# An attention and mixture-of-experts kernel on one core: six items ahead instead of eight, and the start reordered

## The chip, the cores and the metric

The kernel runs on one NeuronCore of a Trainium2 chip. The metric is the device time of one execution in microseconds. Engines are TensorE (PE, with its weight loads PEld), VectorE (DVE), ScalarE (ACT), GpSimd (POOL) and SyncE (SP), which here only issues DMAs.

## What is computed

x is 8 batches of 256 tokens of 128 channels. A layernorm gives xn. One branch is causal attention with 16 heads of 64 channels and rotary position, its keys and values made from a latent of 64 channels; the other is a router over 8 experts, of which each token uses one (hidden size 512, exact gelu). The result joins both.

```python
xn = _layernorm(x)
q = xn @ wq.T
lat = xn @ w_kv_down.T
k, v = lat @ w_k_up.T, lat @ w_v_up.T
s = softmax(causal(rope(q) @ rope(k).T / 8)) @ v @ wo.T
e = max(top2(xn @ gate_w + gate_b))
y = gelu(xn @ w1[e] + b1[e]) @ w2[e] + b2[e]
out = x + s * silu(2 * y)
```

## The kernel before

Every engine has its own program, written out by hand, and all follow one plan (`program`, L266): a start, then 64 slots g, one for each pair of heads of each batch (8 pairs in a batch), and between slots 39 and 40 (`G_LEAD`, L42) the experts, on tokens sorted by expert. Engines meet only at semaphores; each runs its own list in order.

An **item** m is one projection: 8 for each batch, alternately queries (even m) and keys (odd m) of four heads. PE makes it in `project` (L1011; 6 matmuls of 256 columns for queries, 4 for keys, because operands are split in a high and a low part of reduced precision), DVE multiplies it by cosine and sine in `rotate` (L552), POOL adds the two halves into `staged` in `rotated` (L434), and SP moves them with four DMAs for each pair of items (`place`, L343) into `qk_sb`, where the heads lie as the scores need them. One semaphore `qk_in` counts all four DMAs. In slot g PE makes the scores of g + 2 (`scores`, L1027), item g + 8 (`NI` is 8), transposes of the probabilities of g (`turn`, L1039), the output of g - 2 (`output`, L1062) and the values of g - 1 (`values`, L1049). So scores of pair of heads g, made in slot g - 2, need the items up to g + 1. Until slot 19 items use one PSUM bank, later two (`bank_of`, L326), so that a projection waits for the rotation of the item before it, or of the one before that.

In the slot DVE does in this order: row maxima of g + 2 (`row_max`, L559), reciprocals of g + 1, its share of the scaling, whatever stands in `slot` (L745) for that g (statistics in slots 0, 1, 4, 5, 7, 9, normalising of four tiles of tokens in slots 2, 6 and 10, routing in 17 to 22), and last the rotation. POOL scales the probabilities of g + 1 (`scale`, L443; two of the four parts in slots 22 to 37, else all four), adds item g + 8, and in slots 22 to 37 issues one indirect DMA each, which scatters a tile of tokens to its place in the sorted order. In slots 1, 5 and 9 it makes the power for a group of four tiles (`rstd`, L471).

The order on SP (`slot`, L406) is: in slot 39 wait for all scatters, load four tiles of sorted rows (`load`, L401, issue L403), wait for them, load the rest; then the moves, in odd slots; then in slots 1, 3 and 5 the experts' weights (`expert_weights`, L378): w1 in one DMA of 2 MB, w2 in four of 512 KB, b2 with a fill of the sorted array. On PE, `finish` (L1196) ends slot 39's work and transposes the first tile of sorted rows, and `experts` (L1206) waits for the weights, the tile's own weights (copied by POOL, `own_weights`, L516) and the rotations of items up to 47.

In the start (L349, L483, L693, L916, L1136) eight items are projected and rotated. The first four tiles of tokens are normalised and transposed, weights are split in high and low parts (ACT the high, DVE `query_low` L688 and POOL `key_low` L477 the low), value and output weights are multiplied together (`value_output_weights`, L1126), and the moves of items 0 and 1 are issued half by SP and half by ACT.

Of the kernel before, what the change touches and what calls it, by code (L numbers as in the profile page):

```python
# [16 lines left out]
P = 128  # L17
# [23 lines left out]
LEAD = 5  # L41
G_LEAD = LEAD * NP  # L42
# [9 lines left out]
Z_PART = 18  # L52

# [27 lines left out]
def build(nc, x, wqT, w_dgT, w_kupT, w_vup, woT, gate_b, w1, b1, w2, b2,  # L81
          c_rot, c_ident, c_mask, c_before, c_expert, c_excl, c_incl, c_tile, out):
    with ExitStack() as ctx:
# [76 lines left out]
        rstd_all = sb("rstd_all", [P, NT])  # L160
        lg = sb("lg", [P, NT, E])
# [30 lines left out]
        wk_in = [sem(f"wk_in{i}") for i in range(2)]  # L192
        wq_in_done = [sem(f"wq_in{i}") for i in range(2)]
# [11 lines left out]
        rstd_ready = sem("rstd_ready")  # L205
        xn_ready = sem("xn_ready")
# [29 lines left out]
        qk_in = [sem(f"qk_in{i}") for i in range(NG)]  # L236
# [55 lines left out]
        def latents_to(u):  # L292

            t0, t1 = TURNS[u]
            return (bank[1], bank[0], w_bank, w_bank, w_bank)[u][0:DW, 0:(t1 - t0) * P]
# [30 lines left out]
        def bank_of(m):  # L326

            return bank[4 + m % 2] if m < NI or m - NI >= TWO_J else j_bank
# [5 lines left out]
        def place_halves(eng, n, halves):  # L334

            for half in halves:
                for pair in range(2):
                    eng.dma_start(qk_sb[half::2, :, 2 * (n % NG) + pair, :],
                                  staged[HD * pair:HD * pair + HD, n % 2, half]).then_inc(qk_in[n % NG], 16)

        @block.sync
        def _(sp):
            def place(n, halves=(0, 1)):  # L343
# [3 lines left out]
                place_halves(sp, n, halves)  # L347

            def start():  # L349
# [18 lines left out]
                place(0, (0,))  # L368
# [4 lines left out]
                place(3)  # L373
# [4 lines left out]
            def expert_weights(k):  # L378
                if k == 0:
# [3 lines left out]
                    sp.dma_start(w1_view[:, :, 0:FF], w1.rearrange("e c f -> c e f")).then_inc(f_in, 16)  # L383
                    sp.dma_start(w1_view[:, :, FF:FW], b1).then_inc(f_in, 16)
                elif k == 1:
                    for i in range(FB):
# [19 lines left out]
            def slot(g):  # L406
# [26 lines left out]
        def _(pool):  # L433
            def rotated(m):  # L434
# [3 lines left out]
                if n >= 2:  # L438
                    pool.wait_ge(qk_in[(n - 2) % NG], 64 * ((n - 2) // NG + 1))
# [31 lines left out]
            def rstd(u):  # L471
# [3 lines left out]
                pool.tensor_tensor(rstd_all[:, n], veps[:, n], halfneg[:, n], op=ALU.pow).then_inc(rstd_ready, 1)  # L475
# [7 lines left out]
            def start():  # L483
# [7 lines left out]
                key_low(1)  # L491
                key_low(2)
                rotated(0)
                rotated(1)
                key_low(3)
                for m in range(2, 7):
                    rotated(m)
                scale(0)
                rotated(7)

            def slot(g):
                if g + 1 < B * NP and g != G_LEAD:
                    scale(g + 1)
                if g + NI < B * NP:
                    rotated(g + NI)
# [7 lines left out]
            def experts():  # L513
# [15 lines left out]
                pool.wait_ge(f_in, 16 * (2 + FB))  # L529
# [13 lines left out]
        def _(dve):  # L543
# [8 lines left out]
            def rotate(m):  # L552

                dve.wait_ge(proj_done, m + 1)
                wait(dve, staged_ready, m - 1)
# [41 lines left out]
            def variances(u):  # L597

                n = slice(*TURNS[u])
                dve.tensor_scalar(veps[:, n], mv[:, n, 1], LN_EPS, None, ALU.add).then_inc(var_ready, 1)  # L600

            def normalise(u):

                dve.wait_ge(rstd_ready, u + 1)
                for n in range(*TURNS[u]):
# [87 lines left out]
            def start():  # L693
# [9 lines left out]
                normalise(1)  # L703
# [570 lines left out]
```

## Time and profile before

| | us |
|---|---|
| median of 3 runs | 319.66 (319.2 to 320.86) |
| the profiled execution | 319.58 |
| its span, first to last instruction | 317.6 |
| PE busy | 292.8 (92%) |
| ACT busy | 240.7 (76%) |
| DVE busy | 221.0 (70%) |
| POOL busy | 217.4 (68%) |

Times in the rows are microseconds from the start of the span. A row of the timeline gives the start, the duration, the engine and the line, what is written from what, and in brackets how long the engine stood idle before it and who released it. "SPq" is a DMA issue. Slot g begins where PE makes the scores of g + 2 (L1034): slot 0 at 28.99, slot 1 at 31.41, slot 4 at 44.71, slot 39 at 177.22; the experts begin at 183.72.

### The profile page before, as it was taken

How to read it: one execution, taken by the hardware profiler on the slowest of the kernel's cores; microseconds unless marked ns; L12 is line 12 of the kernel's file. 1: busy time of each engine (PE TensorE's matmuls, PEld its weight loads, DVE VectorE, ACT ScalarE, POOL GpSimd, SP SyncE). 2: the span in 40 equal slices, each digit the busy share in tenths (PEclk: the TensorE clock that was granted, in tenths of full speed). 3: DMA queues.
4: the chain of work that ended last, by engine and by line, in shares of the span. 5: the costliest groups of instructions: out<-in, count | busy, mean ns of one | idle time of the engine just before them, and what ended most of it. 6: DMA issues, size and time to landing. Idle time of an engine off the chain costs nothing.

```text
span 317.6 us, 8745 instructions
## 1 busy us (share of the span) xinstructions
PE 292.8 (92%) x2485; PEld 244.6 (77%) x2485; DVE 221.0 (70%) x883; ACT 240.7 (76%) x863; POOL 217.4 (68%) x321
## 2 busy tenths in 40 slices
PE   0878889999999999999999989999999999999984
PEld 0756668787888888888888779999877887886853
DVE  4877898997869698877787522222268789997551
ACT  3226869787887779898999775555699997989972
POOL 3566967778677787999999943333138997899630
PEclk9968999999999999999999999999999999999998
DMA  7537499963333333344433470000063343344200
GB/s 205 188 88 179 105 293 253 311 180 68 67 70 68 67 69 76 86 107 114 104 92 85 107 218 3 0 2 0 2 179 72 87 103 95 101 130 131 59 18 19
DMA packets 39294, 33.37 MB, mean 105 GB/s; under 512 B 4753, under 2 KB 36370, under 8 KB 39250
## 3 DMA queue, kind: packets, MB, share of 16 engines
q1 hardware_dynamic: 37506, 30.24, 36.6%
q0 software_dynamic: 1024, 2.10, 2.6%
q10 hardware_dynamic: 720, 0.50, 0.6%
q8 instruction: 21, 0.34, 0.4%
q14 instruction: 23, 0.19, 0.2%
HBM read 11.07 MB, written 4.98 MB: 51 GB/s over the span
## 4 chain that ended last, share of the span: by engine, by line
PE 73%; issue 8%; DVE 8%; POOL 7%; ACT 2%; DMA 1%; ACTq 1%; POOLq 0%; DVEq 0%
PE bank L1046 11%; PE bank L1034 10%; PE bank L1057 9%; PE bank L1071 8%; PE bank L1235 6%; PE bank L1220 6%; PE bank L1023 4%; PE bank L1036 3%; PE bank L1007 3%; PE bank L1059 3%; POOL staged L440 3%; DVE rot_out L556 3%; PE bank L1024 2%; PE bank L1008 2%; PE bank L1009 2%
## 5 line engine op out<-in xcount | busy, mean ns | idle before, releaser
L852 ACT ACTIVATE pexp<-masked,negmax 128x128 f32<-128x128 f32 (+1 forms) x256 | 114.6, 454 | 3.3 <-DVE negmax L565 3.2
L565 DVE CUSTOM_DVE_ANT_0 masked<-bank,mask 128x128 f32<-128x128 f32 (+1 forms) x256 | 76.0, 353 | 32.4 <-PE bank L1036 32.0
L440 POOL TENSOR_TENSOR staged<-rot_out 128x512 f32<-128x512 f32 x64 | 82.1, 1284 | 23.7 <-DVE rot_out L556 20.8
L451 POOL TENSOR_SCALAR probs<-pexp,rden 128x256 f32<-128x256 f32 (+1 forms) x186 | 80.7, 449 | 23.1 <-DVE rden L572 20.7
L556 DVE TENSOR_TENSOR rot_out<-bank,rot 128x1024 f32<-128x1024 f32 x64 | 77.8, 1215 | 1.5 <-PE bank L1009 0.8
L873 ACT COPY probsT<-bank 128x384 f32<-128x384 f32 x128 | 54.9, 480 | 28.0 <-PE bank L1046 26.8
L1046 PE MATMUL bank<-ident,probs 128*128 128x128 f32 x384 | 53.9, 274 | 0.7 <-POOL probs L451 0.3
L852 ACT ACTIVATION_READ_ACCUMULATOR pexp<-masked,negmax 128x1 f32 x256 | 50.1, 196 | 0.0
L1034 PE MATMUL bank<-qk_sb 64*128 64x256 f32 x256 | 45.5, 432 | 1.9 <-ACT vo_sb L946 1.2
L1046 PEld LDWEIGHTS bank<-ident,probs 128*128 128x128 f32 x384 | 43.2, 140 | 3.0 <-POOL probs L451 1.0
L1071 PE MATMUL bank<-vo_sb,ctxT 128*128 128x128 f32 x256 | 39.9, 278 | 2.7 <-ACT ctxT L879 2.7
L1057 PE MATMUL bank<-probsT,lat_all 128*64 128x256 f32 x256 | 41.8, 404 | 0.3 <-ACT probsT L873 0.3
L991 ACT ACTIVATE hidT<-bank,w_own 128x128 f32<-128x128 f32 x88 | 25.1, 368 | 18.5 <-PE bank L1220 18.4
L1071 PEld LDWEIGHTS bank<-vo_sb,ctxT 128*128 128x128 f32 x256 | 33.8, 191 | 4.3 <-ACT ctxT L879 3.8
L520 POOL COPY w_own<-w_sb 128x516 f32 x22 | 13.5, 616 | 27.3 <-ACT hidT L991 27.3
L1034 PEld LDWEIGHTS bank<-qk_sb 64*128 64x128 f32 x256 | 19.5, 186 | 13.0 <-issue 10.5
L1036 PEld LDWEIGHTS bank<-qk_sb 64*128 64x128 f32 x256 | 25.1, 189 | 3.0
L879 ACT COPY ctxT<-bank 128x256 f32<-128x256 f32 x64 | 23.3, 364 | 4.9 <-PE bank L1059 4.9
L1059 PEld LDWEIGHTS bank<-probsT,lat_all 128*64 128x64 f32 x256 | 18.4, 137 | 9.2
L1235 PE MATMUL bank<-w_sb,hidT 128*128 x176 | 24.4, 282 | 1.0 <-issue 0.5
L1036 PE MATMUL bank<-qk_sb 64*128 64x128 f32 x256 | 25.1, 273 | 0.0
L1059 PE MATMUL bank<-probsT,lat_all 128*64 128x128 f32 x256 | 24.9, 273 | 0.0
(106 smaller groups left out, 457.8 us busy)
## 6 DMA issues: line engine op xcount, KB each, us to landing
qk_sb<-staged SPq DMA_DIRECT2D x126, 128.0 KB
w_sb<-in_w SPq DMA_DIRECT2D x1, 2048.0 KB, 8.7
w_sb<-in_w SPq DMA_DIRECT2D x4, 512.0 KB, 6.2
sorted_x<-z SPq DMA_DIRECT2D x1, 1408.0 KB, 9.9
sorted_g<-z SPq DMA_DIRECT2D x1, 1152.0 KB, 5.9
out<-res SPq DMA_DIRECT2D x8, 128.0 KB
x_sb<-in_x SPq DMA_DIRECT2D x3, 256.0 KB, 3.3
rot<-in_c_rot SPq DMA_DIRECT2D x1, 512.0 KB, 5.8
```

The costliest lines, as they stand in the source:

```text
L440: pool.tensor_tensor(staged[:, n % 2, :, m % 2, :], rot_out[:, m % 2, :, 0:S], rot_out[:, m % 2, :, S:2 * S], op=ALU.add).then_inc(staged_ ...
L451: pool.tensor_scalar(probs[:, g % 2, i, c], pexp[:, g % 2, i, c], rden[:, g % 2, i, k:k + 1], 1.0, ALU.mult, ALU.mult).then_inc(probs_read ...
L556: dve.tensor_tensor(rot_out[:, m % 2], bank_of(m)[:].unsqueeze(1).broadcast_to([P, 2, 2 * S]), rot[:], op=ALU.mult).then_inc(rope_done, 1)
L565: t = dve.tensor_tensor_reduce(masked[:, g % 2, i, c], s_bank[i][:, c], mask[:, c], -1.0, -NEG * 1e8, ALU.add, ALU.min, negmax[:, g % 2, i ...
L852: e = act.activation(pexp[:, g % 2, i, c], masked[:, g % 2, i, c], ACT.Exp, bias=negmax[:, g % 2, i, k:k + 1], scale=-1.0, accum_out=rowsu ...
L873: act.copy(probsT[:, g % 2, i, :], t_bank[i][:, 0:SW]).then_inc(probsT_ready, 1)
L1034: pe.matmul(s_bank[i][:, P:SW], qk_sb[r, 0, p, P:S], qk_sb[r, 1, p, :], start=True, stop=True)
L1036: m = pe.matmul(s_bank[i][:, 0:P], qk_sb[r, 0, p, 0:P], qk_sb[r, 1, p, 0:P], start=True, stop=True)
L1046: t = pe.transpose(t_bank[i][:, k * P:(k + 1) * P], probs[:, g % 2, i, k * P:(k + 1) * P], ident[:])
L1057: pe.matmul(o_bank[r, 0:S], lat_all[:, 2 * b, :], probsT[:, g % 2, i, 0:S], start=True, stop=False)
L1059: m = pe.matmul(o_bank[r, P:S], lat_all[:, 2 * b + 1, :], probsT[:, g % 2, i, S:SW], start=False, stop=True)
L1071: m = pe.matmul(y_bank[:, i * C:(i + 1) * C], ctxT[:, p, i * P:(i + 1) * P], vo_sb[:, p, :], start=(p == 0 and i == 0), stop=(p == NP - 1) ...
```

## The change

Six items are projected in the start (`AHEAD`) instead of eight. In slot g every engine does the items `items(g)`: one, g + 6; but in slots 36 and 38 (`TWICE`) two, so that 48 items are done before the experts, as before. PE does a second item at the end of the slot. `qk_in` becomes one semaphore for each pair of heads, signalled by its two DMAs. All four moves of the first pair are on SP. The expert weights come in pieces of half of w1, or half of w2, in slots 1, 3, 5 and 7, and b2 and the fill in slot 9. In slots 2, 6 and 10 ACT normalises two of the four tiles, from a shift (minus mean times power) that POOL computes behind the power. In the start, PE runs 13 matmuls on ones ahead of everything and 4 behind the first transposes; wq and wk are loaded in three pieces each; item 1 is summed by DVE; the order of the steps is new on each engine; half of the first scaling is DVE's.

```diff
+AHEAD = 6
+TWICE = (36, 38)
+def items(g):
+    ahead = [AHEAD + sum(t < n for t in TWICE) for n in (g, g + 1)]
+    return range(g + ahead[0], min(g + 1 + ahead[1], B * NP))
...
-        qk_in = [sem(f"qk_in{i}") for i in range(NG)]
+        qk_in = [sem(f"qk_in{p}") for p in range(NP)]
...
-            if g >= B * NP - 3:
+            if g == 0 or g >= B * NP - 3:
...
-            return bank[4 + m % 2] if m < NI or m - NI >= TWO_J else j_bank
+            return bank[4 + m % 2] if m < NI or m - AHEAD >= TWO_J else j_bank
...
-            def place(n, halves=(0, 1)):
+            def place(n):
                 sp.wait_ge(staged_ready, 2 * n + 2)
                 wait(sp, scores_done, 2 * n + 2 - NP)
-                place_halves(sp, n, halves)
+                for pair in range(2):
+                    p = 2 * (n % NG) + pair
+                    for half in range(2):
+                        sp.dma_start(qk_sb[half::2, :, p, :],
+                                     staged[HD * pair:HD * pair + HD, n % 2, half]).then_inc(qk_in[p], 16)
...
-                sp.dma_start(rot[:], c_rot).then_inc(rot_in, 16)
-                sp.dma_start(wq_in[:, S:], wqT[:, S:]).then_inc(wq_in_done[1], 16)
-                sp.dma_start(wkup[:, S:], w_kupT[:, S:]).then_inc(wk_in[1], 16)
+                for i in range(1, 3):
+                    c = slice(i * S, (i + 1) * S if i == 1 else H * HD)
+                    sp.dma_start(wq_in[:, c], wqT[:, c]).then_inc(wq_in_done[i], 16)
+                    sp.dma_start(wkup[:, c], w_kupT[:, c]).then_inc(wk_in[i], 16)
+                    if i == 1:
+                        sp.dma_start(rot[:], c_rot).then_inc(rot_in, 16)
...
-                place(0, (0,))
+                place(0)
                 place(1)
                 rows_in(3)
                 place(2)
                 rows_in(4)
-                place(3)
...
-                if g % 2 and g + NI < B * NP:
-                    place((g + NI) // 2)
-                if g in (1, 3, 5):
+                for m in items(g):
+                    if m % 2:
+                        place(m // 2)
+                if g in (1, 3, 5, 7, 9):
                     expert_weights(g // 2)
...
-                pool.tensor_tensor(rstd_all[:, n], veps[:, n], halfneg[:, n], op=ALU.pow).then_inc(rstd_ready, 1)
+                    pool.tensor_tensor(rstd_all[:, n], veps[:, n], halfneg[:, n], op=ALU.pow).then_inc(pool_step, 1)
+                    pool.wait_ge(pool_step, u - 1)
+                    pool.tensor_tensor(shift_all[:, n], negmean[:, n], rstd_all[:, n], op=ALU.mult).then_inc(rstd_ready, 1)
...
                 key_low(1)
+                rotated(0)
                 key_low(2)
-                rotated(0)
-                rotated(1)
+                rotated(2)
+                rotated(3)
                 key_low(3)
-                for m in range(2, 7):
+                for m in range(4, AHEAD - 1):
                     rotated(m)
                 scale(0)
-                rotated(7)
+                rotated(AHEAD - 1)
...
                 turned_low(0)
-                normalise(1)
+                query_low(1)
                 latents_low(0)
                 dve.wait_ge(rot_in, 16)
                 rotate(0)
-                query_low(1)
+                rotate(1)
+                dve.wait_ge(rope_done, 2)
+                dve.tensor_tensor(staged[:, 0, :, 1, :], rot_out[:, 1, :, 0:S], rot_out[:, 1, :, S:2 * S],
+                                  op=ALU.add).then_inc(staged_ready, 1)
+                normalise(1)
+                rotate(2)
                 turned_low(1)
-                rotate(1)
                 query_low(2)
-                rotate(2)
+                rotate(3)
                 latents_low(1)
-                rotate(3)
-                query_low(3)
-                rotate(4)
-                rotate(5)
...
                 row_max(0)
-                rotate(6)
+                rotate(4)
                 row_max(1)
                 denominators(0)
-                rotate(7)
+                scale(0)
+                query_low(3)
+                rotate(5)
                 logits(0)
...
-                    normalise(2)
+                    normalise(2, 2, 4)
...
+                if g in (2, 6, 10):
+                    normalise(g // 4 + 2)
...
-                if p % 2 == 0:
-                    pe.wait_ge(qk_in[p // 2], 64 * (g // NP) + 64)
+                pe.wait_ge(qk_in[p], 32 * (g // NP) + 32)
...
+            def keep_warm(n):
+                for _ in range(n):
+                    pe.matmul(y_bank[:], ones16[:], ones16[:].unsqueeze(1).broadcast_to([P, 4, P]), start=True, stop=True)
...
+                pe.wait_ge(hot_ready, 1)
+                keep_warm(13)
                 pe.wait_ge(id_in, 16)
                 turn_rows(0)
+                keep_warm(4)
                 latents(0)
...
-                if g + NI < B * NP:
-                    project(g + NI)
+                if g < 2:
+                    wait(pe, wq_low if g == 0 else wk_low, 4)
+                for m in items(g)[:1]:
+                    project(m)
...
+                for m in items(g)[1:]:
+                    project(m)
...
-                pe.wait_ge(rope_done, NI * (LEAD + 1))
+                pe.wait_ge(rope_done, items(G_LEAD)[0])
```

PE's start now runs: items 0 to 3, the transposes of tiles 2 and 3, half of the value-output weights, their latents, the other half, scores 0, item 4, scores 1, item 5. ACT's start copies the value-output weights before the first exponentials and turned latents after them. `rotate` and `rotated` are called for `items(g)` on DVE and POOL, as on PE.

## Rows read from the trace of the kernel before

**Rows 1.** Busy time by stretch: stretch, length, PE, PEld, DVE, ACT, POOL, PE clock, DMA share, GB/s.
```profile
10.16:29.00 18.84, 14.14 (x97) 11.31 (x95) 15.39 (x31) 6.26 (x21) 12.45 (x13) 0.82 0.50 129
29.00:49.10 20.10, 17.53 (x149) 14.30 (x149) 17.71 (x83) 15.46 (x58) 16.20 (x29) 1.00 0.71 191
18.60:25.40 6.80, 6.44 (x32) 5.54 (x34) 6.01 (x13) 1.91 (x8) 5.60 (x5) 0.50 0.39 90
128.00:158.00 30.00, 30.00 (x266) 25.05 (x263) 23.13 (x96) 26.74 (x104) 28.17 (x36) 1.00 0.41 104
```

**Rows 2.** Timeline of the start: start, us, engine, line, operation, names, shapes, count.
```profile
5.83 0.41 DVE L685 SCALAR_TENSOR_TENSOR wq_l<-w_sb,wq_h 128x256 fp32r<-128x256 f32 x1
...
8.56 0.41 PE L1007 MATMUL bank<-xnT_h,wq_h 128*128 128x256 f32 x1
...
10.16 1.23 DVE L556 TENSOR_TENSOR rot_out<-bank,rot 128x1024 f32<-128x1024 f32 x1 [0.54 <-PE bank L1009]
...
11.26 1.59 POOL L481 TENSOR_TENSOR wk_l<-w_sb,wk_h 128x256 fp32r<-128x256 f32 x2 [3.17 <-ACT wk_h L914]
11.30 0.97 DVE L685 SCALAR_TENSOR_TENSOR wq_l<-w_sb,wq_h 128x256 fp32r<-128x256 f32 x1
...
12.90 0.28 PE L1008 MATMUL bank<-xnT_l,wq_h 128*128 128x256 f32 x1
...
28.99 0.70 PE L1034 MATMUL bank<-qk_sb 64*128 64x256 f32 x4 [1.17 <-ACT vo_sb L946]
...
29.96 0.29 DVE L565 CUSTOM_DVE_ANT_0 masked<-bank,mask 128x128 f32<-128x128 f32 x1 [0.85 <-PE bank L1036]
```

**Rows 3.** Timeline of slots 1 to 7, the steps around the normalising.
```profile
37.81 1.02 POOL L475 TENSOR_TENSOR rstd_all<-veps,halfneg 128x4 f32<-128x4 f32 x1
...
38.86 1.66 DVE L606 TENSOR_SCALAR xn<-x_sb,mv,rstd_all 128x128 f32<-128x128 f32 x4 [1.19 <-POOL rstd_all L475]
...
41.70 0.38 PE L1023 MATMUL bank<-latT,wk_h 128*128 128x256 f32 x1 [1.43 <-DVE rot_out L556]
...
58.61 0.39 PE L1023 MATMUL bank<-latT,wk_h 128*128 128x256 f32 x1 [0.54 <-DVE rot_out L556]
```

**Rows 4.** Timeline of PE: the first matmuls of slots 36, 37 and 38.
```profile
166.47 0.70 PE L1034 MATMUL bank<-qk_sb 64*128 64x256 f32 x4
...
170.13 0.70 PE L1034 MATMUL bank<-qk_sb 64*128 64x256 f32 x4
...
173.56 0.70 PE L1034 MATMUL bank<-qk_sb 64*128 64x256 f32 x4
```

**Rows 5.** Timeline of POOL before the experts.
```profile
171.73 1.06 POOL L459 DMA_INDIRECT sorted_x<-xn,pos  x1 [0.16 <-issue]
172.83 0.93 POOL L451 TENSOR_SCALAR probs<-pexp,rden 128x256 f32<-128x256 f32 x2
...
176.47 1.62 POOL L451 TENSOR_SCALAR probs<-pexp,rden 128x128 f32<-128x128 f32 x4
...
182.38 1.17 POOL L520 COPY w_own<-w_sb 128x516 f32 x2
```

**Rows 6.** Timeline of SP's queue before the experts, and PE's first transpose of sorted rows.
```profile
175.25 2.55 SPq L338 DMA_DIRECT2D qk_sb<-staged  x4
178.59 3.53 SPq L403 DMA_DIRECT2D z<-sorted_x  x2
...
182.63 0.33 PE L1194 MATMUL bank<-ident,z 128*128 128x128 f32 x1
```

**Rows 7.** Timeline: moves and who waits for them; slot 25's first matmul and its moves.
```profile
21.69 2.98 SPq L338 DMA_DIRECT2D qk_sb<-staged  x4
26.60 1.28 POOL L440 TENSOR_TENSOR staged<-rot_out 128x512 f32<-128x512 f32 x1 [2.26 <-DMA qk_sb<-staged]
...
127.61 0.70 PE L1034 MATMUL bank<-qk_sb 64*128 64x256 f32 x4
133.60 16.40 SPq L338 DMA_DIRECT2D qk_sb<-staged  x12
```

More of the change, by code:

```diff
@@ L191, in build @@
         c_in = sem("c_in")
-        wk_in = [sem(f"wk_in{i}") for i in range(2)]
-        wq_in_done = [sem(f"wq_in{i}") for i in range(2)]
+        wk_in = [sem(f"wk_in{i}") for i in range(3)]
+        wq_in_done = [sem(f"wq_in{i}") for i in range(3)]
         gb_in = sem("gb_in")
@@ L437, in rotated @@
                 pool.wait_ge(rope_done, m + 1)
-                if n >= 2:
-                    pool.wait_ge(qk_in[(n - 2) % NG], 64 * ((n - 2) // NG + 1))
+                for q in (2 * n - 4, 2 * n - 3) if n > 1 else ():
+                    pool.wait_ge(qk_in[q % NP], 32 * (q // NP) + 32)
                 pool.tensor_tensor(staged[:, n % 2, :, m % 2, :], rot_out[:, m % 2, :, 0:S], rot_out[:, m % 2, :, S:2 * S],
@@ L503, in slot @@
                     scale(g + 1)
-                if g + NI < B * NP:
-                    rotated(g + NI)
+                for m in items(g):
+                    rotated(m)
                 if SCATTER_SLOT <= g < SCATTER_SLOT + NT:
@@ L554, in rotate @@
                 dve.wait_ge(proj_done, m + 1)
-                wait(dve, staged_ready, m - 1)
+                wait(dve, staged_ready, max(m - 1, 2) if m > 1 else 0)
                 dve.tensor_tensor(rot_out[:, m % 2], bank_of(m)[:].unsqueeze(1).broadcast_to([P, 2, 2 * S]), rot[:],
@@ L599, in variances, with normalise @@
                 n = slice(*TURNS[u])
+                if u > 1:
+                    dve.tensor_scalar(negmean[:, n], mv[:, n, 0], -1.0, None, ALU.mult)
                 dve.tensor_scalar(veps[:, n], mv[:, n, 1], LN_EPS, None, ALU.add).then_inc(var_ready, 1)
-            def normalise(u):
+            def normalise(u, first=0, last=TQ):
                 dve.wait_ge(rstd_ready, u + 1)
-                for n in range(*TURNS[u]):
+                for n in range(*TURNS[u])[first:last]:
                     dve.tensor_scalar(xn[:, n, :], x_sb[:, n, :], mv[:, n, 0:1], rstd_all[:, n:n + 1],
@@ L806, in slot @@
                     finalise(FINALS[g])
-                if g + NI < B * NP:
-                    rotate(g + NI)
+                for m in items(g):
+                    rotate(m)
             def finish(b):
@@ L902, in latents_copied, with normalise @@
                          src[:, 0:TQ * LAT]).then_inc(lat_copied, 1)
+            def normalise(u):
+                act.wait_ge(rstd_ready, u + 1)
+                for n in range(*TURNS[u])[0:2]:
+                    act.activation(xn[:, n, :], x_sb[:, n, :], ACT.Identity, bias=shift_all[:, n:n + 1],
+                                   scale=rstd_all[:, n:n + 1]).then_inc(xn_ready, 1)
             def query_high(i):
                 c = w_part[i]
-                act.wait_ge(wq_in_done[min(i, 1)], 16)
+                act.wait_ge(wq_in_done[min(i, 2)], 16)
                 act.mul(wq_h[:, c], wq_in[:, c], HD ** -0.5).then_inc(wq_high, 1)
@@ L923, in start @@
                 key_high(0)
+                turned(0)
+                query_high(1)
+                key_high(1)
+                latents_high(0)
+                turned(1)
+                query_high(2)
+                key_high(2)
                 act.wait_ge(id_in, 16)
@@ L1011, in project @@
             def project(m):
-                b, n, g = m // NI, m % NI, m - NI
-                wait(pe, rope_done, m if 0 <= g <= TWO_J else m - 1)
+                b, n, g = m // NI, m % NI, m - AHEAD
+                wait(pe, rope_done, m if m >= NI and g <= TWO_J else m - 1)
                 if g == TWO_J + 1:
@@ L1082, in turn_rows @@
                 for k, n in enumerate(range(*TURNS[u])):
-                    pe.wait_ge(xn_ready, n + 1)
+                    pe.wait_ge(xn_ready, n + 1 if u < 2 else TURNS[u][1])
                     t = pe.transpose(turned_to(u)[:, k * P:(k + 1) * P], xn[:, n, :], ident[:])
```

73 lines of the change are left out of this document (31 added, 42 removed).

## The prediction

> **What bounds the kernel now.** I read four views in this order. The busy time by stretch [rows 1] says where TensorE (PE) is short of work: it is busy 30.00 of 30 us in the middle of the attention slots, but 14.14 of 18.84 in the second part of the start and 17.53 of 20.1 in the first five slots. A microsecond of PE work moved is therefore worth a microsecond in the middle, and next to nothing in the start. The timeline of the start [rows 2] shows what the first slot waits for: its scores go at 28.99, after 8 rotations of 1.23 us on VectorE (DVE) one after the other, and the last release is a copy on ScalarE (ACT). DVE is busy 15.39 of those 18.84 us [rows 1]: it is the engine that paces the start, with 3.45 us idle. The timeline of slots 1 to 7 [rows 3] shows the same engine holding PE: the key projection waits 1.43 us for a rotation at 41.70 and 0.54 us at 58.61, each time because four normalisations (1.66 us) stand ahead of the rotation. The timeline before the experts [rows 5, 6] shows GpSimd (POOL) with hardly a gap (28.17 of 30 us busy in the middle [rows 1]). Some half a per cent, 1.6 us, is what a measurement of this kernel can tell from no change.
>
> The profiled execution took 319.58 us, its span 317.6; the median of the runs shown is 319.66. I make the sum against 319.6.
>
> **1. The start, up to DVE's first slot.** Until the first rotation little moves: DVE follows the arrival of x and POOL's power, both unchanged. The 13 warm-up matmuls run before PE has anything else to do. The products before the first rotation now run at 1.2 GHz, those after it at 2.4: 0.41 and 0.28 us for one of 256 columns [rows 2], of which the columns are 0.21 and 0.11. If the 13 warm-ups of 512 columns all ran at 1.2 GHz they would take 13 × 0.43 = 5.5 us and push the first transposes 0.8 us back; if the clock rises on the way, they end in time. Then the three latent and six query products save about 0.1 each, and the rotation at 10.16 [rows 2] starts at about 9.3, where the table it needs (its load is one of those queued later by 256 KB, some 0.8 us) arrives too.
> From there I add DVE's work. Before: 15.39 us busy to 29.0 [rows 1]. It loses two rotations (2 × 1.23) and a 0.97 us split that now comes before the first rotation; it gains two normalisations moved behind it (0.6), the sum of item 1 (bounded below by half of a 1024-element rotation, 0.6, and above by POOL's time for the same sum, 1.28 [rows 7]; I take 0.65, since a DVE shape is nearer than a POOL one), and half of the first scaling (0.6). That is 13.8 us. Idle time: walking the new order by hand, DVE waits for the first scores, because their moves can only start when two sums are done (at about 12.4) and land 3.2 us later, and again for the second scores; I get 1.3 us. So DVE reaches its first slot at 9.3 + 13.8 + 1.3 = 24.4 where it now gets there at 29.96 [rows 2]: **−5.5 us**. Ends: no idle at all −6.8, all of the present 3.45 us kept −3.3. Two projections taken from PE's start save nothing themselves; PE had 4.7 us free there [rows 1].
> Here the trace has a row on two engines at once: the 256-column split on DVE takes 0.97 us at 11.30 while POOL runs the same kind of subtraction from 11.26, 0.80 each, and 0.41 at 5.83 with POOL idle [rows 2]. The Trainium skill (SBUF — State Buffer, Who interferes with whom) states why: a VectorE instruction with two SBUF inputs and a GpSimd one that reads SBUF lock the same port pair, and the later one waits in full. By that rule DVE's new sum waits for POOL's sum of item 0 beside it, and the start would come out up to 1.3 us later, the sum below at −1.55 in place of −2.85; POOL's sum starts 1.2 us earlier, so I leave it out.
>
> **2. First slots.** Slots 0 to 3 stay paced by DVE, so the shift of 5.5 is kept. Two of the four normalisations of each group go to ACT: 0.83 us off DVE, and about 0.2 us back for POOL's extra small product that both now wait for (no row has it; between 0.1 and the 1.02 of the power beside it [rows 3]). In slot 2 that gives another **−0.3** once PE is no longer waiting for the rest, and in slots 6 and 10 it removes the wait of 0.54 us [rows 3]: **−1.1** for the two. ACT has the room (15.46 busy of 20.1 [rows 1]). The expert weights come as 1 MB at a time behind the moves of every second slot instead of 2 MB at once; nobody waits for them now, so nothing there.
>
> **3. The two projections come back.** In slots 36 and 38 PE does one projection more, a key and a query one. An even slot (query, 6 matmuls) lasts 3.66 us and an odd one (key, 4) 3.43 [rows 4]: 0.115 per matmul, so 0.46 + 0.69 = **+1.15**, in full on the path.
>
> **4. What the extra sums do to POOL and to SP's queue.** This is the term the diff hides. POOL has no gap in slots 35 to 37: a scatter issue (1.06), two scalings (0.93), one sum (1.28 [rows 5, 7]). Now slot 36 has two sums, and the second waits for a rotation of a projection that PE does last in its slot, at 170.7 in the old times, rotated by 172.0: the scatter at 171.73 [rows 5] goes to 173.5, the next to 176.9. In slot 38 come the four scalings (1.62 [rows 5]) and then both sums, 45 and 46. The moves of item pair 22 wait for sum 45; they went at 175.25 [rows 6] and now go at about 180.9. They are ahead of the load of sorted rows on SP's queue: four issues, 2.55 us [rows 6], so the load that went at 178.59 goes at 183.5 and lands at 186.2. PE transposed its first tile at 182.63 [rows 6] and with the 1.15 of part 3 would want it at 183.8: **+2.4**. The second load waits for the first, which adds about **+0.5** at the second tile. POOL's weight copy, 182.38 [rows 5], goes to about 185.1; it is covered by that wait. Ends: nothing, if POOL has slack I don't see; +4 if the walk is a microsecond short.
>
> **Sum:** −5.5 − 0.3 − 1.1 + 1.15 + 2.4 + 0.5 = −2.85; **316.8 us**.
>
> **Rivals.** (a) The clock falls again. It was at half from 18.6 to 25.4, with PE busy 6.44 of 6.8 us [rows 1]. There is no warm-up work after the first products, and PE still has pauses between them. In the new order what lies on the path from there to DVE's first slot is one projection and two sets of scores, some 1.6 us more: 318.4. (b) POOL and SP keep up before the experts: part 4 is nothing, 313.9. For it: POOL's period is a little below PE's, so it may have more lead by slot 36 than the rows show. (c) The start's idle time doesn't shrink, because the moves and splits that DVE waits for only change places: −3.3 in place of −5.5, 319.0; the change then does not do what it says. (d) Slower: with six items ahead the moves come too late. An odd slot's moves must be down three slots later, 3.43 + 3.66 + 3.43 = 10.52 us [rows 4]. In slot 37 they start 5.1 us after the slot [rows 4, 6]; landing took 1.9 us after the last issue (24.67 to 26.60, [rows 7]), so a first pair is down 3.2 after its start: 8.3. But in slot 25 they start 6.0 us after it (127.61 to 133.60 [rows 7]), beside a scatter. If landings under scatters take 1.5 us more, each of some eight pairs in slots 23 to 37 holds PE by 0.5 to 1; at 2 us more it is about 8 × 1.0 = 8 us, and the time 324. It decides from 1.3 us more. Against it: the signal is now by pair, so the second pair's landing no longer counts.
>
> **Chances.** Forecast 0.40, (a) 0.20, (b) 0.20, (c) 0.12, (d) 0.08. Faster by over 0.5% means under 318.1: nearly all of the forecast, a third of (a), all of (b), hence 0.67. Within 0.5%: 0.25. Slower by over 0.5%: 0.08, (d). The range goes from (b) to (c) with the bounds of parts 1 and 4: 313.5 to 319.6. It leaves out (d) and the outer ends of the others.
>
> **What would show it.** Right: scores of slot 0 near 22 and of slot 4 near 39; a half-clock row gone or not tells (a); no wait in slots 7 and 11; the load of sorted rows nearly 5 us later against slot 36 than now, with PE's first expert transpose waiting for it. Wrong: PE waiting for moves in even slots from 24 on (d), a load that goes right after the last scatter (b), slot 0 at 24 or later at full clock (c).

## The result: 1.6 us faster, where 2.8 had been forecast

| | before | changed |
|---|---|---|
| median of 10 runs each, us | 319.43 (318.29 to 320.86) | 317.87 (317.22 to 318.16) |
| the profiled execution | 319.58 | 317.84 |

The ratio is 0.9953, 95% interval 0.9938 to 0.9968: faster by 1.56 us, just under half a per cent. The first slot starts 7.6 us earlier, and four fifths of that are lost again by the time the experts end. The first lines of the page of the changed kernel:

```profile
span 316.1 us, 8823 instructions
PE 296.5 (94%) x2502; PEld 244.6 (77%) x2502; DVE 217.2 (69%) x883; ACT 243.0 (77%) x869; POOL 215.9 (68%) x321
```

PE is busier (296.5 us for 292.8) though its work is the same but for the 17 warm-up matmuls, whose products nobody uses. The account is best kept by the time at which PE begins a slot, which is a row of its timeline (L1064 for L1034 before). Negative numbers are the change against before.

| slot | 0 | 4 | 13 | 36 | 39 | 40 |
|---|---|---|---|---|---|---|
| before | 28.99 | 44.71 | 82.91 | 166.47 | 177.22 | 230.07 |
| changed | 21.37 | 37.75 | 74.99 | 158.56 | 170.88 | 228.60 |
| difference | -7.62 | -6.96 | -7.92 | -7.91 | -6.34 | -1.47 |

So there are three stretches to explain: a gain of 7.9 up to slot 13, a loss of 1.6 in slots 36 to 38, and a loss of 4.9 from slot 39 to 40, where the experts lie. After slot 40 nothing changes.

**The start.** Timeline of the changed kernel, from its first matmuls to DVE's first slot; it answers to [rows 2]:

```profile
1.10 5.67 PE L1169 MATMUL bank<-ones 128*128 128x512 bf16 x13 [1.10 <-DVE ones L716]
...
9.42 2.35 DVE L576 TENSOR_TENSOR rot_out<-bank,rot 128x1024 f32<-128x1024 f32 x2
...
10.72 1.28 POOL L454 TENSOR_TENSOR staged<-rot_out 128x512 f32<-128x512 f32 x1 [1.91 <-DVE rot_out L576]
...
11.81 0.75 DVE L731 TENSOR_TENSOR staged<-rot_out 128x512 f32<-128x512 f32 x1
...
14.46 0.41 DVE L707 SCALAR_TENSOR_TENSOR wq_l<-w_sb,wq_h 128x256 fp32r<-128x256 f32 x1
14.55 0.91 POOL L500 TENSOR_TENSOR wk_l<-w_sb,wk_h 128x256 fp32r<-128x256 f32 x1 [2.54 <-ACT wk_h L945]
...
21.37 0.70 PE L1064 MATMUL bank<-qk_sb 64*128 64x256 f32 x4 [1.00 <-DVE negmax L585]
...
21.94 0.41 DVE L707 SCALAR_TENSOR_TENSOR wq_l<-w_sb,wq_h 128x256 fp32r<-128x256 f32 x1
...
23.50 0.27 DVE L585 CUSTOM_DVE_ANT_0 masked<-bank,mask 128x128 f32<-128x128 f32 x1
```

The first rotation goes at 9.42 for 10.16, and DVE reaches the row maximum of its first slot at 23.50 for 29.96. Each split of a query weight takes 0.41 us on DVE, where those of before took 0.97, 0.73 and 1.30. Busy time by stretch, with the columns of [rows 1]:

```profile
9.42:23.50 14.08, 11.78 (x102) 9.53 (x103) 12.74 (x34) 8.23 (x29) 7.77 (x8) 1.00 0.65 174
```

DVE is busy 12.74 of these 14.08 us and idle 1.34. The granted clock (the column before the last two, as a share of 2.4 GHz) is 1.00 throughout; before, it was 0.50, which is 1.2 GHz or half clock, from 18.6 to 25.4.

**Slots 2 to 7**, timeline, answering to [rows 3]:

```profile
30.12 0.38 PE L1038 MATMUL bank<-xnT_h,wq_h 128*128 128x256 f32 x1 [1.13 <-DVE rot_out L576]
...
31.39 1.02 POOL L492 TENSOR_TENSOR rstd_all<-veps,halfneg 128x4 f32<-128x4 f32 x1
...
32.48 0.20 POOL L494 TENSOR_TENSOR shift_all<-negmean,rstd_all 128x4 f32<-128x4 f32 x1
...
32.72 0.88 ACT L932 ACTIVATE xn<-x_sb,shift_all,rstd_all 128x128 f32<-128x128 f32 x2 [0.34 <-POOL shift_all L494]
32.72 0.84 DVE L628 TENSOR_SCALAR xn<-x_sb,mv,rstd_all 128x128 f32<-128x128 f32 x2 [1.46 <-POOL shift_all L494]
...
34.74 0.38 PE L1054 MATMUL bank<-latT,wk_h 128*128 128x256 f32 x1 [0.88 <-DVE rot_out L576]
...
51.18 0.39 PE L1054 MATMUL bank<-latT,wk_h 128*128 128x256 f32 x1
```

PE's wait in slot 3 is 0.88 for 1.43, and that of slot 7 is gone. But DVE now stands 1.46 us for POOL's small product, where it stood 1.19 for the power.

**Slots 36 to 40**, timeline, answering to [rows 4 to 6]: PE's first matmuls of slots 36 to 39, POOL, SP's queue, and PE's two waits behind:

```profile
158.56 0.70 PE L1064 MATMUL bank<-qk_sb 64*128 64x256 f32 x4
...
162.89 0.70 PE L1064 MATMUL bank<-qk_sb 64*128 64x256 f32 x4
...
166.55 0.70 PE L1064 MATMUL bank<-qk_sb 64*128 64x256 f32 x4
...
169.19 1.06 POOL L473 DMA_INDIRECT sorted_x<-xn,pos  x1 [0.17 <-issue]
...
170.29 1.62 POOL L465 TENSOR_SCALAR probs<-pexp,rden 128x128 f32<-128x128 f32 x4
...
170.88 0.70 PE L1064 MATMUL bank<-qk_sb 64*128 64x256 f32 x4
...
171.89 2.51 POOL L454 TENSOR_TENSOR staged<-rot_out 128x512 f32<-128x512 f32 x2
...
173.19 2.55 SPq L354 DMA_DIRECT2D qk_sb<-staged  x4
...
175.78 3.83 SPq L416 DMA_DIRECT2D z<-sorted_x  x2
...
178.86 0.75 SPq L416 DMA_DIRECT2D z<-sorted_x  x1
178.93 0.30 PE L1231 MATMUL bank<-ident,z 128*128 128x128 f32 x1 [2.56 <-DMA z<-sorted_x]
...
187.63 1.15 PE L1272 MATMUL bank<-w_sb,hidT 128*128 x8 [1.35 <-ACT hidT L1022]
```

Slots 36 and 38 last 4.33 us each. The load of sorted rows goes at 175.78, 4.90 us after the start of slot 39 (before: 178.59, 1.37 after it), right behind the four moves; PE waits 2.56 us for it. The second load, of the remaining rows, is issued at 178.86, once the first has landed, and lands 8.6 us later, at 187.5. The product of the second tile (`experts`, where t is 1) waits in the program for both loads; it goes at 187.63, and the ACT operation that it needs had ended at 185.4. So this wait of 1.35 us is for the second load. Between the two waits the granted clock falls for a while:

```profile
176.30:180.70 4.40, 1.45 (x12) 1.25 (x11) 0.77 (x3) 2.54 (x6) 2.91 (x6) 0.99 0.44 107
180.70:184.10 3.40, 3.02 (x15) 2.57 (x13) 0.29 (x1) 1.14 (x4) 1.37 (x3) 0.50 0.95 281
```

### The profile page after: what moved, and what is told of

The parts are those of the page before. It is cut to its first block, busy times and chain, and to the rows that moved or that the text cites. A ratio compares the mean times of both kernels' runs of the same rounds, so it can differ in the third digit from the quotient of the medians.

```text
span 316.1 us, 8823 instructions
## 1 busy us (share of the span) xinstructions
PE 296.5 (94%) x2502; PEld 244.6 (77%) x2502; DVE 217.2 (69%) x883; ACT 243.0 (77%) x869; POOL 215.9 (68%) x321
## 4 chain that ended last, share of the span: by engine, by line
PE 63%; DVE 11%; issue 11%; POOL 10%; ACT 2%; DMA 2%; SPq 1%; POOLq 0%; DVEq 0%; ACTq 0%
PE bank L1076 9%; PE bank L1064 8%; PE bank L1087 7%; PE bank L1101 6%; PE bank L1257 6%; PE bank L1272 6%; POOL staged L454 5%; DVE rot_out L576 4%; DVE masked L585 3%; POOL probs L465 3%; PE bank L1038 3%; PE bank L1089 3%; PE bank L1066 3%; PE bank L1054 2%; PE bank L1169 2%
## 5 line engine op out<-in xcount | busy, mean ns | idle before, releaser
L454 POOL TENSOR_TENSOR staged<-rot_out 128x512 f32<-128x512 f32 x63 | 80.4, 1277 | 23.9 <-DVE rot_out L576 23.3
L1064 PE MATMUL bank<-qk_sb 64*128 64x256 f32 x256 | 45.0, 428 | 2.7 <-DVE negmax L585 2.5
L1064 PEld LDWEIGHTS bank<-qk_sb 64*128 64x128 f32 x256 | 19.4, 184 | 13.7 <-issue 12.6
L1257 PE MATMUL bank<-xsT,w_own 128*128 128x128 f32 x176 | 24.7, 286 | 0.8 <-DVE xsT L845 0.8
```

The lines of the kernel that those rows point to most:

```text
L454: pool.tensor_tensor(staged[:, n % 2, :, m % 2, :], rot_out[:, m % 2, :, 0:S], rot_out[:, m % 2, :, S:2 * S], op=ALU.add).then_inc(staged_ ...
L1064: pe.matmul(s_bank[i][:, P:SW], qk_sb[r, 0, p, P:S], qk_sb[r, 1, p, :], start=True, stop=True)
L1257: m = pe.matmul(bank[4 + o][:, k * P:(k + 1) * P], w1_own[:, o, k * P:(k + 1) * P], xsT[:, o, :], start=True, stop=True)
```

## The experiments

Twelve kernels were run, in five rounds each beside the kernel before, whose median was 319.3 to 320.1. Starts of slots and times, in us:

| kernel | slot 0 | slot 13 | slot 39 | slot 40 | median (lowest to highest) | ratio to before, 95% |
|---|---|---|---|---|---|---|
| e1 loads first | 21.53 | 75.17 | 171.05 | 224.33 | 313.75 (313.11 to 314.02) | 0.9810 (0.9781 to 0.9839) |
| e2 catch up at 20, 22 | 21.39 | 75.01 | 171.10 | 225.39 | 314.27 (313.71 to 314.64) | 0.9823 (0.9794 to 0.9852) |
| e3 warm in the wait | 21.02 | 74.66 | 170.54 | 227.60 | 317.31 (316.87 to 317.56) | 0.9924 (0.9899 to 0.9949) |
| e4 normalise on DVE | 21.33 | 77.36 | 173.25 | 230.32 | 319.74 (319.15 to 321.56) | 1.0011 (0.9991 to 1.003) |
| e5 e1, no warm-ups | 22.54 | 76.20 | 172.08 | 225.51 | 314.64 (313.77 to 315.88) | 0.9846 (0.9818 to 0.9875) |
| e6 e1, item 1 on POOL | 22.57 | 77.08 | 172.96 | 226.35 | 315.19 (313.69 to 315.80) | 0.9849 (0.9818 to 0.9880) |
| e7 e1 and e2 | 21.11 | 74.74 | 170.82 | 224.38 | 313.88 (313.61 to 314.07) | 0.9823 (0.9799 to 0.9847) |
| e8 before, warm-ups | 26.67 | 81.22 | 175.53 | 228.34 | 318.67 (317.53 to 320.18) | 0.9971 (0.9951 to 0.9992) |
| e9 before, ACT moves nothing | 27.08 | 81.01 | 175.31 | 227.97 | 317.54 (316.04 to 319.00) | 0.9929 (0.9905 to 0.9952) |
| e10 e1, eight ahead | 24.56 | 77.77 | 172.07 | 225.66 | 315.16 (314.12 to 315.78) | 0.9849 (0.9814 to 0.9885) |
| e11 e1, power first | 21.59 | 74.13 | 170.01 | 223.44 | 312.44 (312.09 to 313.12) | 0.9767 (0.9734 to 0.9800) |
| e12 e1, weights whole | 21.32 | 78.33 | 174.21 | 227.76 | 314.33 (313.90 to 317.01) | 0.9822 (0.9790 to 0.9854) |

### e1: the loads of sorted rows ahead of the moves

```diff
                     load(4, NR)
+                    for m in items(g - 1):
+                        if m % 2:
+                            place(m // 2)
                 for m in items(g):
-                    if m % 2:
+                    if m % 2 and g != G_LEAD - 2:
                         place(m // 2)
```

> SP issues the two loads of sorted rows ahead of the moves of items 44 and 45, no other edit. Theory (the queue: moves ahead of the loads, and the second load sets when the second tile's product may go): the first load goes within 1 us of the last scatter's landing, about 172.5 instead of 175.8, PE waits at most 0.3 us before the first transposed tile, the clock stays at full, slot 40 comes 3 us earlier than in the changed kernel: about 314.8 us in all. Rival (POOL is what is late; its copies of the experts' weights bind): the load moves but PE then waits for the weight copy at 177.8 instead, and at most 1 us is won: 317. Rival (the half clock costs the time, and comes from something other than the wait): the clock row stays and less than 1 us is won.

313.75 us, 4.1 less than the changed kernel. Timeline:

```profile
171.72 3.46 SPq L416 DMA_DIRECT2D z<-sorted_x  x2
...
175.28 7.53 SPq L354 DMA_DIRECT2D qk_sb<-staged  x8
176.47 0.33 PE L1234 MATMUL bank<-ident,z 128*128 128x128 f32 x1
...
178.12 1.13 PE L1260 MATMUL bank<-xsT,w_own 128*128 128x128 f32 x8 [0.41 <-POOL w_own L543]
```

The load goes 0.67 us after slot 39's start, PE's transpose waits for nothing, its clock stays at 2.4 GHz, and slot 39 to 40 takes 53.28 us for 57.72 (before: 52.85). The order on one issue queue is worth 4.4 us here; what is left over before is 0.4, the wait for POOL's weight copy. The second load goes at 174.43 and lands 7.0 us later, 1.9 before PE's product of the second tile wants it, so it holds nothing. The time is 1 us under the forecast.

### e2: the two extra items in slots 20 and 22

```diff
-TWICE = (36, 38)
+TWICE = (20, 22)
```

> The two extra items are projected in slots 20 and 22 instead of 36 and 38. Theory (POOL has no slack in the slots with scatters, and has some before them): the two sums are absorbed before slot 36, the loads stand to slot 39 as in the kernel before, and the end is at 319.6 - 7.9 + 1.2 to 1.6 = about 313 us. Rival (the extra items cost wherever they are, since DVE has its routing work in slots 17 to 22): stalls of 1 to 3 us in slots 20 to 24, 315 to 317. Rival (a later start of the scatters in slot 22 keeps POOL late to the end): about 316.

314.27 us. POOL and SP catch up before the scatters, the load goes at 172.34, and slot 39 to 40 takes 54.29. The two extra projections cost the same in either place: slot 39 starts at 171.10 for 170.88. PE still waits 0.75 us for this load, which takes 5.0 us from its issue to the transpose, for 3.15 in the changed kernel, and then 0.89 us for the second load. The forecast of 313 left out both.

### e3: warm-up matmuls in the wait for the load

```diff
                     pe.wait_ge(masked_ready, 2 * G_LEAD + 4)
+                    for _ in range(11):
+                        pe.matmul(bank[1][:], ones16[:],
+                                  ones16[:].unsqueeze(1).broadcast_to([P, 4, P]), start=True, stop=True)
                     pe.wait_ge(xs_in, 16)
```

> PE runs 11 matmuls on ones (about 2.4 us at full clock, into a bank that is free) while it waits for the first load; the loads stay where they are. Theory (the second load sets the time of the second tile's product): the clock stays at full and the first tiles go faster by 1.5 us, but the second product waits that much longer, and the time stays within 0.3 us of the changed kernel, 317.6 to 318.2. Rival (the fall of the clock is what costs): about 1.4 us faster, 316.4.

317.31 us, 0.56 less than the changed kernel; slot 39 to 40 takes 57.06 us, 0.66 less. The granted clock is 1.00 throughout, and PE comes to the second tile's product earlier, but then waits for the second load all the same:

```profile
186.63 1.15 PE L1274 MATMUL bank<-w_sb,hidT 128*128 x8 [0.90 <-issue]
```

So the theory on the second load holds: in the changed kernel PE's slower work at half clock is hidden in front of that landing. The 0.66 us come from the landing itself: it is 7.0 us after the issue, for 8.6, but the issue is 0.8 us later, because the first load took that much longer (transpose 3.94 us after its issue, for 3.15). Without that delay the quicker landing would be worth about 1.4. Over all profiled executions the second load landed 6.8 to 7.1 us after its issue, except in the changed kernel (8.6) and e4 (8.2), the only two with half clock at that place. That the clock makes the load slower is not shown.

### e4: all four tiles normalised on DVE

The slots' `normalise(u, 2, 4)` on DVE take all four tiles, ACT none; POOL's shift stays.

> DVE normalises all four tiles of each group again, ACT none; POOL still computes the shift. Theory (the share that ACT took removes PE's wait of 0.54 us in slots 7 and 11 and some of that in slot 3): slots 7 and 11 have their wait back, slot 13 begins about 1.5 us later than in the changed kernel (74.99), and the end is about 1.5 us later, 319.4. Rival (ACT's share only moves work; the wait was covered by the first slots' chain): less than 0.4 us.

319.74 us, 1.9 more than the changed kernel and as slow as the kernel before. Slot 13 starts 2.37 us later, in three steps of 0.8 (slots 3, 7 and 11). In slot 3 PE waits twice as long as with the work shared:

```profile
35.50 0.39 PE L1053 MATMUL bank<-latT,wk_h 128*128 128x256 f32 x1 [1.68 <-DVE rot_out L576]
```

In slots 7 and 11 it waits 0.79 us each, for 0.54 in the kernel before and nothing in the changed one.

### e5 and e8: the warm-up matmuls, taken away and added

e5 is e1 without both calls of `keep_warm`; e8 is the kernel before with both.

> The kernel with the loads first (313.75 us), without the 13 and the 4 warm-up matmuls. Theory (the clock in the start is a part of the gain): the first rotation begins at about 10.1 instead of 9.4, and the clock falls to half for a stretch of the start as in the kernel before; DVE paces the start, so only the two scores and projections on its path get longer: 1.5 to 2.5 us slower in all, about 315.8. Rival (the order alone made the gain, the clock none): within 0.7 us, the shift of the first rotation. Rival (the clock made most of it): over 4 us slower.

> The kernel before with the 13 and the 4 warm-up matmuls at the same places, nothing else. Theory (the old order has its own waits on ACT and DVE, the clock is a lesser part): the first rotation at 9.4 instead of 10.16, no half-clock stretch, slot 0 about 1.5 to 2.5 us earlier than 28.99, the time about 317.4. Rival (the clock made most of the 7.6 us that the start won): slot 0 at 24 or earlier, 314 or so. Rival (nothing, as the clock falls all the same behind the warm-ups): within 0.8 us.

Without them e1 takes 314.64 us, 0.9 more: slot 0 starts 1.0 later. Its products of 256 columns still take 0.41 us at 13.00, the pace of 1.2 GHz, and 0.28 from 15.9 on, where e1 has 0.28 from 8.5 us on. (The granted clock of the profile reads 1.00 in this stretch too; the pace is read from the durations.) The half-clock stretch that was forecast does not come: the granted clock stays at 1.00 up to 309. With them the kernel before takes 318.67, a ratio of 0.9971 or 0.9 us less (slot 0 starts 2.3 us earlier in the profiled execution, which at 317.76 is one of the fastest of twelve). DVE's first rotation goes at 8.98 for 10.16 there, and the half-clock stretch is shorter (19.0 to 22.4). So the warm-ups give about a microsecond in either kernel, and e1 has no half-clock stretch in the start with them or without.

### e6: item 1 summed by POOL

```diff
-                dve.wait_ge(rope_done, 2)
-                dve.tensor_tensor(staged[:, 0, :, 1, :], ...).then_inc(staged_ready, 1)
...
                 rotated(0)
+                rotated(1)
                 key_low(2)
```

> The kernel with the loads first, with item 1's two halves added by POOL behind item 0's instead of by DVE. Theory (the sum on DVE lets the first moves start early, at the price of 0.75 us of DVE): the first moves start 0.75 us later (POOL ends at 13.3), DVE is 0.7 us ahead until it waits for the first scores; slot 0 within 0.5 us, either way. Rival (the first moves set the start): slot 0 0.8 us later or more.

Not settled. The six executions lie at 313.7 and 313.9, with a mean granted clock of 1.00, and at 314.9 to 315.8 (four), with 0.987 to 0.994. In the profiled one, of the second group, slot 0 starts 1.04 us later than in e1: PE waits 2.21 us for moved items there, where it waits 0.99 for DVE in e1, and the clock is at 1.2 GHz from 22.2, near the end of that wait, to 29.0. So slot 0 is late by what the rival asked for, but not for its reason: SP's first four moves go at 12.77 for 12.74, and in the second four one issue takes 1.61 us, the others 0.6. Why that one is long is not known. In the two executions of the first group the time is that of e1, so there DVE's sum neither costs nor gives more than a few tenths.

### e7: e1 and e2 together

> Loads first and the extra items in slots 20 and 22. Theory (what was left of e2_twice_20_22 is the second load, which waits for moves issued ahead of the first; with these behind it the experts start as in the kernel with loads first, and the earlier items cost 0.2 us more before slot 39): 313.6 to 314.0, the same as loads first alone. Rival (POOL is still late with the extra sums at 36 and 38, and its slack counts now): 0.5 us or more faster than 313.75.

313.88 us for 313.75: nothing on top. Once the loads go first, what POOL and SP still owe is behind them and costs nothing.

### e9: the kernel before with ACT issuing no moves

```diff
-                place(0, (0,))
+                place(0)
...
-                act.wait_ge(staged_ready, 2)
-                place_halves(act, 0, (1,))
```

> The kernel before, with all four moves of items 0 and 1 issued by SP and none by ScalarE. Theory (in the start before, ScalarE stands 5.44 us idle in front of the copy of the latents at 17.23 because its queue holds two moves that wait for both staged items, and VectorE then waits 2.11 us for that copy at 17.63): the copy goes as soon as its matmul is done, near 14, VectorE's wait of 2.11 goes, slot 0 starts about 2 us earlier (near 27) and the time is near 317.5. Rival (the moves themselves pace the start: with four issues on one queue the last lands some 1.3 us later, and TensorE at half clock has its own work to do): slot 0 moves by less than 0.5 us and the time stays within 0.5 us of the kernel before.

317.54 us. In the kernel before, the timeline has:

```profile
15.55 1.63 ACTq L338 DMA_DIRECT2D qk_sb<-staged  x2
...
17.23 0.37 ACT L889 CAST latT<-bank 64x256 fp32r<-64x256 f32 x1 [5.44 <-issue]
...
17.63 0.42 DVE L619 TENSOR_TENSOR latT<-bank,latT 64x256 fp32r<-64x256 f32 x1 [2.11 <-ACT latT L889]
```

and in e9:

```profile
13.72 0.37 ACT L889 CAST latT<-bank 64x256 fp32r<-64x256 f32 x1 [2.11 <-PE bank L1007]
...
15.42 5.90 SPq L338 DMA_DIRECT2D qk_sb<-staged  x8
```

The copy goes 3.5 us earlier, DVE no longer waits for it, slot 0 starts 1.9 us earlier, and the time falls by 0.7%, or 2.3 us. (Half clock lasts from 20.2 to about 23.7 here, for 18.6 to 25.4; what share of the gain that is was not tried.) Two DMAs on an engine's queue, waiting for items of other engines, had held the engine's own work.

### e10: eight items ahead again

```diff
-AHEAD = 6
-TWICE = (36, 38)
+AHEAD = 8
+TWICE = ()
```

with items 6 and 7 projected and rotated in the start, and their moves, on e1.

> The changed kernel with the loads of sorted rows ahead of the last moves (as e1_loads_first), eight items ahead instead of six, and so no slot with two projections. Theory (the start is paced by VectorE's work; rotations of items 6 and 7, 1.2 us each, come back into it, and the two extra projections in slots 36 and 38 cost 1.6 us): slots from 4 to 36 start about 2.4 us later than with six, 1.6 us come back by slot 40, and the time is 314.5 against 313.75. Rival 1 (the number ahead is most of what the change gains in the start, through the wait chain and not only the two rotations): more than 3 us slower, 317 or over. Rival 2 (the start has room on VectorE and TensorE for both): the slots start where they start with six, and the time is 312.2.

315.16 us, 1.4 over e1. Slots 4 to 36 start 2.60 us later (161.33 for 158.73 at slot 36), and 1.58 come back in slots 36 and 38. The edit changes the number ahead alone, but its price has the clock in it: before item 6 PE waits 1.91 us for the split query weights, and half clock lasts from the end of that wait, 22.1, to 25.5. Five of the six executions have a mean granted clock of 0.986 to 0.994 and take 314.6 to 315.8; the one with 0.998 takes 314.12, 0.4 over e1.

### e11: POOL's power ahead of the sum

```diff
+                if g in (1, 5, 9):
+                    rstd(2 + g // 4)
                 for m in items(g):
                     rotated(m)
...
-                if g in (1, 5, 9):
-                    rstd(2 + g // 4)
```

> As e1_loads_first, with POOL's power and its small product for the next four tiles issued ahead of that slot's sum, in slots 1, 5 and 9, in place of behind it. Theory (in slot 2 VectorE waits 1.46 us for that small product at 32.72, and TensorE 0.88 us for the rotation behind it at 34.74): both waits go, slots from 4 on start 0.9 to 1.4 us earlier, and the time is near 312.6 against 313.75. Slots 6 and 10, where TensorE did not wait, give nothing. Rival (POOL has no slack: the sum that now stands behind 1.2 us of power holds the moves and the next rotation, and TensorE waits as long at another place): slot 13 starts within 0.3 us of where it does in e1_loads_first, and so does the end.

312.44 us, the best kernel of the study: 2.3% under the kernel before, or about 7.5 us. Timeline of slots 1 to 3:

```profile
29.84 1.01 POOL L495 TENSOR_TENSOR rstd_all<-veps,halfneg 128x4 f32<-128x4 f32 x1
...
30.93 0.20 POOL L497 TENSOR_TENSOR shift_all<-negmean,rstd_all 128x4 f32<-128x4 f32 x1
31.08 1.27 POOL L457 TENSOR_TENSOR staged<-rot_out 128x512 f32<-128x512 f32 x1
...
31.40 1.38 DVE L631 TENSOR_SCALAR xn<-x_sb,mv,rstd_all 128x128 f32<-128x128 f32 x2
...
34.00 0.39 PE L1057 MATMUL bank<-latT,wk_h 128*128 128x256 f32 x1
```

DVE's wait of 1.46 and PE's of 0.88 are gone; slot 4 starts 0.91 earlier than in e1 and slot 13 1.04.

### e12: the expert weights whole

w1 as one DMA of 2 MB in slot 1, the four of w2 in slot 3, the rest in slot 5.

> As e1_loads_first, with the expert weights loaded as in the kernel before: w1 as one DMA of 2 MB in slot 1, the four of w2 in slot 3, the rest in slot 5. Theory (with six ahead instead of eight the moves of slots 3 and 5 have only three slots to land, and they queue behind bursts of 2 MB): TensorE stalls up to 1.5 us in slots 6 to 10 waiting for a moved item, slot 13 starts that much later, and the time is 313.8 to 315. Rival (loading in pieces changes nothing that anyone waits for, as forecast): no wait for a move in slots 4 to 12, slot 13 and the time within 0.3 us of e1_loads_first.

314.33 us, 0.6 over e1. The timeline shows the moves of slot 5 behind the four DMAs of w2, and PE's wait for them in slot 8:

```profile
42.39 5.38 SPq L397 DMA_DIRECT2D w_sb<-in_w  x4
47.87 3.65 SPq L354 DMA_DIRECT2D qk_sb<-staged  x4
```

```profile
55.91 0.70 PE L1064 MATMUL bank<-qk_sb 64*128 64x256 f32 x4 [1.69 <-DMA qk_sb<-staged]
```

In the profiled run, the slowest of the seven at 317.01 (the others take 313.9 to 314.9, so their wait or what follows it must be smaller), this wait is followed by half clock:

```profile
57.50:60.90 3.40, 3.40 (x16) 2.92 (x14) 2.43 (x16) 1.43 (x3) 2.48 (x5) 0.50 1.07 303
```

So loading in pieces matters with six ahead. The kernel before loads whole with eight ahead, and in its trace PE waits for no move: there the moves had two slots more.

## Why the prediction was right, and where its sizes were off

The direction, the steps and their places were right; the parts came to -1.5 at slot 40 for a forecast of -2.85. That it is no further off is in part luck: the start gained 1.0 us more than forecast, and the stretch before and in the experts lost 2.4 more.

**Part 1, forecast -5.5 at DVE's first slot, measured -6.5.** The first rotation (9.3 forecast, 9.42) and the idle time (1.3 forecast, 1.34) were right. The term that was mis-sized is DVE's work, 13.8 forecast and 12.74 measured. It kept the splits of query weights at the durations of before, 0.73 and 1.30 us; they took 0.41 each, 1.2 less in all. By the Trainium skill (SBUF — State Buffer, Who interferes with whom) the one of two such instructions that comes later waits. The rows agree on which: at 14.46 DVE's split came 0.09 us ahead of POOL's and took 0.41, POOL's 0.91, for 0.75 in the next one at 17.87. That is 0.16 longer, where a wait in full would be 0.32. DVE's new sum came while POOL's ran (to 12.00) and took 0.75; it lost at most 0.19 us to it, so the 1.3 that the rule could have cost here did not appear. That the result is near the -1.55 which the prediction gave for that case is a coincidence: the loss came from part 4.

What the gain of 7.6 us at slot 0 is made of, by experiments taken one at a time: two items fewer in the start 3.0 (e10, with a half-clock stretch in it), ACT's queue 1.9 (e9), the warm-ups 1.0 (e5). These were taken on different kernels and need not add up. What is left, 1.7, was not taken apart: the new order of the steps (with it the shorter splits, 1.2 us of DVE), the loads of wq and wk in three pieces, and the moves signalled by pair. The prediction had not seen ACT's queue: its rows of the start did not include the 5.44 us that ACT stood idle, and DVE's wait of 2.11 us for it was hidden in "3.45 us idle". Rival (a), the clock falling again in the start, and rival (c), the idle time staying, did not come in the profiled execution.

**Part 2, forecast -0.3 and -1.1, measured -0.5 and -0.96.** From DVE's first slot to slot 4 the difference goes from -6.46 to -6.96; from there to slot 13 to -7.92, half of it in slots 6 and 7. The small product took 0.20 us as forecast. But the same work moved back costs 2.4 (e4), not 1.4, because POOL's small product stays in e4: the waits in slots 7 and 11 are 0.25 longer than before, and that in slot 3 is 1.68 for 1.43. So e4 prices ACT's share, not the difference from the kernel before. The prediction put the loading of the weights in pieces at nothing. As a difference that was right, but with six ahead the pieces are what keeps it at nothing (e12).

**Part 3, forecast +1.15, measured +1.57.** A slot with a second projection lasts 4.33 us; 0.67 and 0.90 more, for 0.46 and 0.69 forecast. So each has 0.2 us above the price of its matmuls, of a cause that was not looked for.

**Part 4, forecast +2.9, measured +4.9.** The walk through the queues held nearly to the tenth. In the old times (7.91 us added) the moves go at 181.1 (forecast 180.9), the load at 183.7 (183.5), and PE waits 2.56 us for it (2.4). The term that was mis-sized is "the second load ... adds about +0.5": it adds 2.3. What holds PE is the landing of the second load, and from the start of slot 39 it goes like this. It is issued 8.0 us on, for 4.1 before: 3.9 later. It lands 8.6 us after its issue, for 6.9 before: 1.7 more. Before, it landed 0.8 us ahead of the product that wants it. Together 4.8, and that product goes 4.9 later. With a landing as before the sum would be 3.1, near the 2.9 forecast, so the missing 1.7 is the slower landing, which the prediction took as unchanged; its cause stays open. The half clock from 180.7 to 184.1 adds nothing of its own in this trace, because PE then still waits 1.35 us for the same landing; e3, without it, waits 0.90. Rival (b) is what e1 and e2 make true: 313.75 and 314.27, for 313.9 forecast.

**Rival (d)**, moves too late, shows in e12 (1.69 us in slot 8), and a late move also holds slot 0 in e6; in the changed kernel PE's longest wait for a move before slot 39 is 0.19 us, in slot 2.

## What to carry to other kernels

Before work is moved into the slots ahead of a hand-over, write down what stands in front of the next phase's first load on its issue queue: here four small moves that no one reads until slot 42, over 50 us on, stood ahead of a load that PE needed at once, and they took back 4.4 of 7.9 us. A second transfer that waits for the first can be what binds: follow it to its landing too. Look for the same on every engine that issues DMAs beside its own work, where the profile shows it as idle time with "issue" as its cause. An engine's wait for a small operation of another (1.2 us of POOL behind a 1.3 us sum) can be had for a change of order alone.

## What was unexpected in the hardware

- The granted clock fell to 1.2 GHz not only in the start but behind single waits of PE: 180.7 to 184.1 after a wait of 2.56 us, and 57.5 to 60.9 after one of 1.69 (e12). In the start it fell towards the end of a wait of 2.21 (e6, 22.2 to 29.0) and of one of 1.91 (e10, 22.1 to 25.5). In e3, with most of the wait filled, it did not fall. Executions of one kernel differ in it: e6 has two groups of times, 313.7 to 313.9 at a mean granted clock of 1.00 and 314.9 to 315.8 at 0.987 to 0.994, and e12's profiled run is 2.7 us over its median.
- 13 warm-up matmuls of 512 columns took 5.67 us in the changed kernel, 0.44 each, the pace of the lower level, and 5.26 in e1. In e1 they pushed the first transposes from 5.71 (e5) to 6.20; still DVE's first rotation came 0.2 us earlier with them (9.58 for 9.79).
- The first load of sorted rows landed 3.0 us after its issue in the changed kernel, 4.9 in e2 and 2.6 in e1, though e1 issued it earliest after the start of slot 39 (0.7 us, for 1.2 in e2 and 4.9 in the changed kernel). So how soon it follows the scatters does not explain it, and the cause is open.
